# The last experts' second product with the hidden units as the stationary operand, and another order of TensorE's round

## The reference

```python
def _L1_ffn_ref(x, router_w, router_b, W1, b1, W2, b2):
    # B, K, D = 128, 16, 64; E = 32 experts; H = 16 units each
    xf = x.reshape(-1, D)
    logits = xf @ router_w.T + router_b
    idx = jnp.argmax(logits, axis=-1)
    h = jnp.einsum('nd,ndh->nh', xf, jnp.take(W1, idx, axis=0)) + jnp.take(b1, idx, axis=0)
    h = jax.nn.relu(h)
    out = jnp.einsum('nh,nhd->nd', h, jnp.take(W2, idx, axis=0)) + jnp.take(b2, idx, axis=0)
    return jax.nn.relu(out).reshape(x.shape)
```

## Time and profile before

| | us |
|---|---|
| median of 3 runs (1122.95 to 1123.62) | 1123.39 |
| the profiled execution's own time | 1124.06 |
| its span, first to last instruction | 1121.9 |
| PE busy in the span | 987.0 |
| DVE / ACT / POOL busy in the span | 698.7 / 663.6 / 516.3 |
| the last phase, from its first instruction on PE at 1001.02 to the span's end | 120.9 |

### The profile page before, as it was taken

The page is one execution under the profiler, slowest core; times in us unless marked ns, Lnnn a source line. Parts: engine busy times, 40 slices in busy tenths (PEclk is TensorE's granted clock), DMA queues, the critical chain, the costliest instruction groups (busy, mean ns, idle before and its releaser), DMA issues.

```text
span 1121.9 us, 34992 instructions
## 1 busy us (share of the span) xinstructions
PE 987.0 (88%) x12202; PEld 677.4 (60%) x12202; DVE 698.7 (62%) x1954; ACT 663.6 (59%) x1224; POOL 516.3 (46%) x812
## 2 busy tenths in 40 slices
PE   3789876688869799999999998699999999949998
PEld 0245444466647587777777777266666666635555
DVE  3356652577747556766667675288888888844443
ACT  1134543477755567676767673377777777635554
POOL 0001101577747367676767765245555555441110
PEclk9989996599989899999999998599999999979999
DMA  8432100000000000000000000000000000000001
GB/s 243 74 58 38 19 1 1 1 1 0 0 1 1 1 3 3 1 0 0 0 0 0 0 2 2 1 2 3 0 0 0 0 0 0 1 1 15 19 19 25
DMA packets 10769, 14.99 MB, mean 13 GB/s; under 512 B 9296, under 2 KB 9296, under 8 KB 9680
## 3 DMA queue, kind: packets, MB, share of 16 engines
q1 hardware_dynamic: 10704, 14.13, 5.9%
HBM read 12.03 MB, written 2.10 MB: 13 GB/s over the span
## 4 chain that ended last, share of the span: by engine, by line
PE 53%; issue 11%; POOL 7%; DVE 7%; ACT 2%; POOLq 1%; DVEq 0%; ACTq 0%
PE ps L1758 6%; PE ps L1331 5%; PE ps L1343 5%; POOL e_acc L1273 5%; PE ps L1780 4%; PE ps L1766 4%; PE ps L1748 3%; PE ps L1922 3%; PE ps L1746 3%; PE ps L1955 3%; DVE a_rmax L1804 2%; DVE a_diff L1807 2%; PE ps L1105 1%; PE ps L608 1%; PE ps L789 1%
## 5 line engine op out<-in xcount | busy, mean ns | idle before, releaser
L1540 ACT ACTIVATE e_hid<-ps,cst 128x512 f32<-128x512 f32 x256 | 161.6, 682 | 78.4 <-PE ps L1331 78.4
L1343 PEld LDWEIGHTS ps<-ew,e_hid 128*64 128x64 f32 x4096 | 130.0, 138 | 42.4 <-issue 29.1
L1273 POOL TENSOR_TENSOR e_acc<-e_acc,e_part 128x512 f32<-128x512 f32 x96 | 123.6, 1288 | 64.8 <-DVE e_part L1478 64.6
L1478 DVE TENSOR_TENSOR e_part<-ps,e_wt 128x512 f32<-128x512 f32 x128 | 88.4, 691 | 99.1 <-PE ps L1343 77.0
L1343 PE MATMUL ps<-ew,e_hid 128*64 128x64 f32 x4096 | 147.6, 225 | 0.0
L1331 PE MATMUL ps<-e_xs,ew 64*128 64x256 f32 x1024 | 146.7, 406 | 0.0
L1804 DVE TENSOR_REDUCE a_rmax<-ps 128x8 f32<-128x1024 f32 x64 | 78.2, 1222 | 38.2 <-PE ps L1758 37.1
L1331 PEld LDWEIGHTS ps<-e_xs,ew 64*128 64x128 f32 x1024 | 89.3, 188 | 16.0 <-issue 2.5
L1713 POOL TENSOR_TENSOR a_sum<-a_part 128x256 f32<-128x256 f32 x64 | 46.5, 727 | 108.1 <-DVE a_part L1815 108.1
L204 POOL TENSOR_TENSOR t_prob<-t_ex,t_rscale 128x512 f32<-128x512 f32 x8 | 12.0, 1502 | 172.2 <-DVE t_rscale L377 172.2
L1766 PEld LDWEIGHTS ps<-cst,a_ex 128*128 128x128 f32 x512 | 55.6, 141 | 50.6 <-issue 41.5
(11 more groups left out here) (260 smaller groups left out, 2035.7 us busy)
## 6 DMA issues: line engine op xcount, KB each, us to landing
x_in<-x_dram SPq DMA_DIRECT2D x48, 128.0 KB, 4.7
cst<-cst_dram SPq DMA_DIRECT2D x1, 3037.0 KB, 16.9
out_dram<-e_res SPq DMA_DIRECT2D x16, 128.0 KB, 1.9
ew<-ew_dram SPq DMA_DIRECT2D x1, 1024.0 KB, 18.9
cst<-cst_dram SPq DMA_DIRECT2D x1, 704.0 KB, 7.4
ew<-ew_dram SPq DMA_DIRECT2D x1, 512.0 KB, 20.4
cst<-cst_dram SPq DMA_DIRECT2D x1, 329.5 KB, 3.1
```

What stands on the lines that cost most here:

```text
L1273: eng.tensor_tensor(acc[:, :, :, :], acc[:, :, :, :], part[n % RING][:, :, :, :], ALU.add).then_inc(sum_sb.sem, 1)
L1343: mm = eng.matmul(m.ps[rows, 6 + n % 2, to:to + C], hid[e % 4][:, a:a + C], w2[:, e * C:e * C + C], start=True, stop=True)
L1478: eng.tensor_tensor(part[n % RING][:, :, :, :], m.ps[:, 6 + n % 2, :].rearrange("p (s j c) -> p s j c", s=TS, j=2), wt[b][:, :, 2 * n:2 * ...
L1540: nc.scalar.activation(hid[e % 4][:, :].rearrange("p (r t) -> p r t", r=2), m.ps[:, 2 + 2 * (n % 2):4 + 2 * (n % 2), j * 256:(j + 1) * 256 ...
```

## The change

- `out` has its operands exchanged: `hid[c][:, a:a+C]`, 128 units by 64 tokens, is stationary and `fw2`'s 64 columns stream past. The result is in token order at once, in bank 5: four chunks times four samples times two halves, 32 matmuls of 64 columns.
- The bias products become `biases`, a step of their own in the same form (8 matmuls), ahead of `turn_hot` and `out`.
- `back_to_tokens`, `e_halves`, its ACT copy, its semaphores and the constant `eye2` are gone.
- `logits(g)` goes ahead of `hidden(g-1)`, and no longer waits for `res_sb`. In `hidden` all eight mask products go ahead of all eight unit products.
- The copy to `e_hotT` moves from ACT to DVE, behind `e_closed`.

```diff
     def pe(eng):
         def logits(g, b):
             eng.wait_ge(T.xs_sb.sem, T.xs_sb.at(g))
-            eng.wait_ge(res_sb.sem, res_sb.at(g - 2))
             eng.wait_ge(hotT_sb.sem, hotT_sb.at(g - 1))
...
         def hidden(g, b):
+            eng.wait_ge(closed_sb.sem, closed_sb.at(g))
             eng.wait_ge(hid_sb.sem, hid_sb.at(g - 1))
...
+            for n in range(2):
                 for r, rows in enumerate(HALVES):
+                    c = 2 * n
+                    eng.matmul(m.ps[:, 1 + 2 * n + r, 0:256], sel[rows, c * P:(c + 1) * P], closed[rows, :],
+                               start=True, stop=False)
+                    c = 2 * n + 1
+                    eng.matmul(m.ps[:, 1 + 2 * n + r, 256:512], sel[rows, c * P:(c + 1) * P], closed[rows, :],
+                               start=False, stop=False)
+            for c in range(NC):
                 for r, rows in enumerate(HALVES):
+                    mm = eng.matmul(m.ps[:, 1 + 2 * (c // 2) + r, (c % 2) * 256:(c % 2 + 1) * 256],
+                                    m.cst[rows, a + c * P:a + (c + 1) * P], T.xs[b][rows, :], start=False, stop=(c % 2 == 1))
+                if c % 2:
+                    mm.then_inc(hid_ps.sem, 1)
...
-        def out(g, b):
-            a = AT["fw2"][0]
-            eng.wait_ge(half_sb.sem, half_sb.at(g - 1))
+        def biases(g, b):
             eng.wait_ge(hotT_sb.sem, hotT_sb.at(g))
...
             for s in range(TS):
                 for rows in HALVES:
+                    a = s // 2 * P + rows.start
+                    eng.matmul(m.ps[rows, 5, s * C:(s + 1) * C], hotT[b][:, a:a + C], col(m, f"fb2{s % 2}"),
+                               start=(s == 0), stop=False)
+
+        def out(g, b):
+            at = AT["fw2"][0]
+            for c in range(NC):
+                eng.wait_ge(hid_sb.sem, hid_sb.at(g, c + 1))
+                for s in range(TS):
+                    for rows in HALVES:
+                        a = place(s) * P + rows.start
+                        mm = eng.matmul(m.ps[rows, 5, s * C:(s + 1) * C], hid[c][:, a:a + C],
+                                        m.cst[:, at + c * C:at + (c + 1) * C], start=False,
+                                        stop=(c == NC - 1 and s == TS - 1))
             mm.then_inc(out_ps.sem, 1)
 
         def rest(g, b, left, back):
-            if back:
-                hidden(g - 1, 1 - b)
             if left is not None:
                 logits(g, b)
+            if back:
+                hidden(g - 1, 1 - b)
             if left:
                 T.pe(eng, g + 1, 1 - b)
             if back:
-                out(g - 1, 1 - b)
+                biases(g - 1, 1 - b)
             if left is not None:
                 turn_hot(g, b)
             if back:
-                back_to_tokens(g - 1, 1 - b, None if left is None else g)
+                out(g - 1, 1 - b)
...
             eng.tensor_scalar(closed[:, :], m.ps[:, 7, 0:NT // 2], -1.0, None, ALU.add).then_inc(closed_sb.sem, 1)
+            eng.wait_ge(out_ps.sem, out_ps.at(g - 2))
+            eng.tensor_copy(hotT[b][:, :], m.ps[:, 7, 0:NT // 2]).then_inc(hotT_sb.sem, 1)
...
-            if back:
-                eng.wait_ge(half_ps.sem, half_ps.at(g - 1))
-                eng.wait_ge(out_ps.sem, out_ps.at(g - 2))
-                nc.scalar.activation(halves[:, :], m.ps[:, 5, :], ACT.Identity).then_inc(half_sb.sem, 1)
-            if left is not None:
-                eng.wait_ge(closed_sb.sem, closed_sb.at(g))
-                eng.wait_ge(half_ps.sem, half_ps.at(g - 2))
-                nc.scalar.activation(hotT[b][:, :], m.ps[:, 7, 0:NT // 2], ACT.Identity).then_inc(hotT_sb.sem, 1)
```

More of the change, by code:

```diff
@@ L53 @@
 COLS += [("routw", EXPERTS1), ("routbr", EXPERTS1), ("iota32", EXPERTS1), ("fw1", HID1), ("fb1", 4),
-         ("fw2", 4 * C), ("fb20", C), ("fb21", C), ("sel32", HID1), ("eye2", C)]
+         ("fw2", 4 * C), ("fb20", C), ("fb21", C), ("sel32", HID1)]
 NCOL = sum(w for _, w in COLS)
@@ L1877, in experts1 @@
     hid = [sb(f"hid{n}", [P, NT]) for n in range(NC)]
-    halves = sb("halves", [P, NT])
     res = [sb(f"res{b}", [P, TS, C]) for b in range(2)]
@@ L1884, in experts1 @@
     hid_ps, hid_sb = step("hid_ps", 2), step("hid_sb", NC)
[L1885 removed]
+    out_ps, res_sb = step("out_ps"), step("res_sb")
     stored = [ctx.enter_context(nc.semaphore(f"out_stored{b}")) for b in range(2)]
@@ L1915, in hidden @@
         def hidden(g, b):
+            eng.wait_ge(closed_sb.sem, closed_sb.at(g))
             eng.wait_ge(hid_sb.sem, hid_sb.at(g - 1))
             a = AT["fw1"][0]
-            def units(n, k, **flags):
-                c = 2 * n + k
+            for n in range(2):
                 for r, rows in enumerate(HALVES):
[L1922 to L1927, removed]
-                for r, rows in enumerate(HALVES):
[L1929 to L1934, removed]
-                    eng.wait_ge(closed_sb.sem, closed_sb.at(g))
-                shut(n, 0, start=False, stop=True)
-                shut(n, 1, start=True, stop=False)
-                units(n, 1, start=False, stop=True).then_inc(hid_ps.sem, 1)
+                    c = 2 * n
[5 more added lines that the diff above has]
+            for c in range(NC):
+                for r, rows in enumerate(HALVES):
+                    mm = eng.matmul(m.ps[:, 1 + 2 * (c // 2) + r, (c % 2) * 256:(c % 2 + 1) * 256],
+                                    m.cst[rows, a + c * P:a + (c + 1) * P], T.xs[b][rows, :], start=False, stop=(c % 2 == 1))
+                if c % 2:
+                    mm.then_inc(hid_ps.sem, 1)
         def turn_hot(g, b):
@@ L1962, in back_to_tokens @@
-        def back_to_tokens(g, b, later):
-            eng.wait_ge(half_sb.sem, half_sb.at(g))
             eng.wait_ge(res_sb.sem, res_sb.at(g - 1))
-            if later is not None:
-                eng.wait_ge(logit_sb.sem, logit_sb.at(later))
             for s in range(TS):
                 for rows in HALVES:
-                    a = place(s) * P + rows.start
-                    mm = eng.matmul(m.ps[rows, 6, s * C:(s + 1) * C], halves[:, a:a + C], col(m, "eye2"),
-                                    start=True, stop=True)
+                    a = s // 2 * P + rows.start
@@ L1972, in back_to_tokens @@
             mm.then_inc(out_ps.sem, 1)
         def rest(g, b, left, back):
+            if left is not None:
+                logits(g, b)
             if back:
                 hidden(g - 1, 1 - b)
-            if left is not None:
-                logits(g, b)
             if left:
@@ L2029, in result @@
             eng.wait_ge(stored[b], store_value(g, b))
-            eng.scalar_tensor_tensor(out=res[b][:, :, :], in0=m.ps[:, 6, 0:TS * C].rearrange("p (s c) -> p s c", s=TS),
+            eng.scalar_tensor_tensor(out=res[b][:, :, :], in0=m.ps[:, 5, 0:TS * C].rearrange("p (s c) -> p s c", s=TS),
                                      scalar=0.0, in1=m.h[:, bass.ds(g * TS, TS), :], op0=ALU.max,
@@ L2288, in more_constants @@
     put("fb20", f1("b2")), put("fb21", f1("b2"), 64)
-    put("eye2", np.concatenate([np.eye(C, dtype=np.float32)] * 2))
     for row in (0, 64):
```

3 lines of the change are left out of this document (removed).

## The result

| | before | after |
|---|---|---|
| first comparison: median | 1123.17 us (4 runs, 1120.87 to 1123.62) | 1105.28 us (4 runs, 1105.1 to 1105.58) |
| ratio | | 0.9845, 95% interval 0.9828 to 0.9862 |
| the profiled execution's own time | 1124.06 | 1105.45 |
| all runs of the two unedited kernels: median | 1117.8 us (60 runs, 1112.4 to 1124.05) | 1105.3 us (8 runs, 1100.9 to 1107.9) |

The kernel is faster, by more than I said: 17.9 us in the first comparison against 13.1, and 1105.28 lies 0.7 under my range. The last row says why that needs care: with more runs the difference of the medians is 12.5 us. The 95% interval knows only the scatter within those eight runs, and the runs of the kernel before alone scatter over more.

The account below looks back on a forecast made before the run. PE was taken as the bound, with 6.5 us of work and about 0.4 of waiting for ACT a round. Savings of 11.0 + 0.6 + 1.5 = 13.1 us from 1123.39 gave 1110.3 us, range 1106.0 to 1114.5.

Parts of the forecast that it names:

- The exchanged product at 2.06 us, the biases at 0.57, the turn at 0.36: PE's new steps each round: 2.99 us together against 3.84 for the steps they replace, 0.85 less a round.
- L1970's gross price: Rival for product and biases: short records cost 39 ns, not 31, giving 1117.3 us; chance 9 in 100.
- Units, mask and logits 2.74 in another order: PE's 32 reordered records in each round would take 2.74 us again, give or take 0.1.
- No new wait in a round: In each round PE would wait for neither DVE nor ACT; the one-hot would be ready 0.27 us in time.
- A round of 6.09, 11.0 us over rounds 2 to 14: Loop rounds on PE: 2.74 + 0.36 + 2.99 = 6.09 us each, saving 13 x 0.85 = 11.0 us.
- Round 15 in 5.8, round 16 in 5.0: The last two rounds: 5.8 us from 6.41, saving 0.6, and 5.0 us from 6.51, saving 1.5.
- Round 1: nothing: First round: logits now wait for `e_hotT` until 1007.6; no gain or loss was counted.
- Sum 13.1: Total saving over the last phase's rounds: 11.0 + 0.6 + 1.5 = 13.1 us.
- 1123.39 - 13.1 = 1110.3, and 0.2% is what a measurement of this kernel can tell: Whole kernel: the saving taken from the median of the runs gives 1110.3 us; 0.2% is 2.2 us.
- the clock's rise 0.5 us in round 1: Uncertainty allowed for when the clock rises: 0.5 us, one of the terms behind 1108.5 to 1112.5 us.

Follow-up runs that it names:

- the pair that starts at 998.01: Profiled executions of the unedited kernel before, run again (1115.34 us), and the changed kernel with 64 unused constant columns (1103.52 us); both reach the one-hot's first turn at 998.01.
- clock_fill: Changed kernel plus seven pairs of idle matmuls where PE waits at the start of the second attention; median 1102.7 us of 4 runs.
- halves_apart: Changed kernel with the loops over samples and halves exchanged in `out`, four matmuls of one half in a row; median 1114.7 us of 10 runs.

## Why the prediction was right in its mechanism and wrong in its number

By its own steps:

- *The exchanged product at 2.06 us, the biases at 0.57, the turn at 0.36.* Measured 2.01, 0.62 and 0.37: 3.00 against 2.99. The rows of L1343 and L1359 were the right ones, and L1970's gross price was not. A record took 31 ns, each with its own load (1024 records of PE and 1024 of PEld in L1955), and even with the halves apart 41.
- *Units, mask and logits 2.74 in another order.* 1049.79 - 1047.05 = 2.74.
- *No new wait in a round.* True; the router had 0.58 us to spare, where I gave it 0.27, as its chain took 2.43 from `e_logit` to the end of `e_hot`, not 2.59.
- *A round of 6.09, 11.0 us over rounds 2 to 14.* (1089.75 - 1010.45) / 13 = 6.10, so 13 x 0.83 = 10.8.
- *Round 15 in 5.8, round 16 in 5.0.* 1095.49 - 1089.75 = 5.74 and 1100.37 - 1095.49 = 4.88.
- *Round 1: nothing.* Mis-sized: neither pair of traces shows it. From the turn to round 2 it took 1015.99 - 1006.02 = 9.97 before and 1010.45 - 999.72 = 10.73 after, 0.8 us more; in the pair that starts at 998.01 it took 9.30 and 10.51, 1.2 more. The wait for `e_hotT` was as I had it, and logits, mask and units took 5.26 us (1001.35 to 1006.61) at a granted clock of 0.50, where the same work took 5.27 before. What I had too cheap lies behind them: I priced L608 and the biases at 0.36 and 0.57, from rows at a granted clock of 1.00, and they took 0.62 and 0.84 (1006.61 to 1007.23 to 1008.07), since the granted clock rose from 0.50 only at 1007.8, within the biases. How late it rises differs between executions: 8.0 us after the turn here and 5.4 in `clock_fill`, where the same code took 9.54.
- *Sum 13.1.* The first pair of traces shows 12.3: 10.8 in rounds 2 to 14, 0.7 in round 15, 1.6 in round 16, less 0.8 in round 1. With 1.2 for round 1 my sum is 11.9, and the pair that starts at 998.01 shows 11.8.
- *1123.39 - 13.1 = 1110.3, and 0.2% is what a measurement of this kernel can tell.* This step failed. I took three runs that lay within 0.7 us as the kernel's time and its spread. The kernel's runs go from 1112.4 to 1124.05, a spread of 1%, and 1123.39 is near the top of it; the changed kernel's first four runs then lay at its own middle. Of the 18.6 us between the two profiled executions 6.3 lie ahead of the changed code, and a second execution of the unchanged kernel reached that code 8.0 us sooner than the first. Median to median of all runs the difference is 12.5 us. From the median of all runs, which I didn't have, the forecast would have been 1117.8 - 13.1 = 1104.7, close to the 1105.3 measured. I gave the clock's rise 0.5 us in round 1 alone and nothing in the four other stretches at a granted clock of 0.50. The 0.5 was my estimate and no run shows it; the runs showed up to 1.2 us in the last phase and 2.2 in the second attention. That the profiled execution's mean clock was 0.943 was in the profile; that it could be 0.952 was in no trace that I had.

What stays open: why one set of runs can lie within 0.7 us while another of the same kernel spreads over 12, and which of the stretches ahead of the second attention give the larger part of the scatter.

## What to carry to other kernels

A product that gives its result in the wrong layout can be cheaper with its operands exchanged although the product itself isn't: what pays is the turn back (0.62 us a round here) and the wait for the copy in between (0.4), against 0.24 more for the product. Price it from a product of the same form in the same trace, from start to start, and keep the two halves of the output in turn (31 ns a record here, against 41 apart). A gain of about 1% in a program with stretches at a granted clock of 0.50 (five of 10 us or more here) is read from the trace of the changed phase, or from two executions that reached it at the same time, since the times themselves differed by as much with no change at all (1112.4 to 1124.05).

## What the runs showed of the hardware that was not expected

- Short float32 matmuls of 64 columns, written to one half of the output's partitions, cost 41 ns a record (82 a matmul) with four of one half in a row, and 31 when the halves alternate: not a factor of two (`halves_apart` 2.62 us for 64 records, the changed kernel 2.01).
- One change less from one form of matmul to another made a round about 0.15 us shorter (two pairs of transposes 0.73 apart and 0.59 together; the round 6.10 and 5.95).
- The scatter of one unchanged program was 12 us of 1118, with a difference of 2.2 us in a stretch where the granted clock was 0.50, and 14 matmuls of idle work in that stretch brought the phase from 309.0 or 311.2 us to 305.1 (305.2 in the second execution with them).
